# Group norm moments aggregated chunk by chunk, mean squares on ScalarE, sum completed in TensorE's average

## What is computed

```python
diff = a1 - lam * a2
out = einsum(diff, v)                      # B, H, T, 64
mean = mean(out, axis=(1, 3)); var = var(out, axis=(1, 3))   # per sequence and head
out = (out - mean) * rsqrt(var + EPS) * gn_w + gn_b
out = out.reshape(B, T, 1024) * (1 - LAMBDA_INIT) @ Wo
x = layernorm(x + out); ...                # then the experts
```

## Time and profile before

| | |
|---|---|
| median of 3 runs | 2042.45 us |
| the runs | 2035.61 to 2043.52 us |
| the profiled execution's own time | 2053.17 us |
| its span in the trace | 2051.3 us |
| mean granted TensorE clock | 0.925 |
| batches 1 to 7 in the attention stage | about 160 us each |

### The profile page before, as it was taken

How to read it: one execution, slowest core, us unless ns; L and a number is a source line. 1 busy time by engine, 2 the same in 40 slices (tenths; PEclk the granted TensorE clock), 3 DMA queues, 4 the chain that set the end, 5 groups by cost and what they waited for, 6 DMA issues and landing times. The chain is left out here.

```text
span 2051.3 us, 36805 instructions
## 1 busy us (share of the span) xinstructions
PE 1706.9 (83%) x9698; PEld 1270.7 (62%) x9699; DVE 1389.8 (68%) x3225; ACT 1166.7 (57%) x3378; POOL 585.5 (29%) x480
## 2 busy tenths in 40 slices
PE   4578899899889889889889889783999999999600
PEld 3355666666656656656665666442999999999600
DVE  2589888888888988888888898734333333333385
ACT  2478788688777877777877877822222222222133
POOL 2232232432331331242242242011633342100173
PEclk8799999999999999999999999975999999999855
DMA  7975574574474474575466565113543344433285
GB/s 253 294 210 141 137 194 121 161 213 114 143 209 134 143 216 125 137 215 153 136 206 165 145 189 150 54 69 140 165 125 118 92 133 151 128 102 93 78 270 194
DMA packets 142469, 318.74 MB, mean 155 GB/s; under 512 B 16720, under 2 KB 19408, under 8 KB 140272
## 3 DMA queue, kind: packets, MB, share of 16 engines
q1 hardware_dynamic: 112272, 238.98, 41.6%
q0 software_dynamic: 15072, 50.74, 7.4%
q10 hardware_dynamic: 14976, 27.27, 3.5%
HBM read 215.21 MB, written 109.05 MB: 158 GB/s over the span
## 5 line engine op out<-in xcount | busy, mean ns | idle before, releaser
L806 ACT ACTIVATE expd<-S,neg_max 128x128 f32<-128x128 f32 (+3 forms) x1024 | 531.5, 536 | 161.2 <-DVE neg_max L961 159.0
L961 DVE TENSOR_REDUCE neg_max<-S 128x2 f32<-128x768 f32 (+3 forms) x384 | 399.9, 1041 | 164.9 <-PE S L650 155.9
L992 DVE SCALAR_TENSOR_TENSOR mixed<-expd,rho 128x384 f32<-128x384 f32 (+3 forms) x512 | 335.4, 675 | 0.0
L646 PE MATMUL S<-kT,qT 128*128 128x256 f32 (+2 forms) x1024 | 278.5, 374 | 20.7 <-ACT expd L806 11.2
L818 ACT ACTIVATE probsT<-PTp 128x512 f32<-128x512 f32 (+2 forms) x384 | 205.2, 534 | 114.7 <-PE PTp L661 112.8
L661 PE MATMUL PTp<-ident,mixed 128*128 128x128 f32 x1280 | 215.8, 284 | 53.5 <-DVE mixed L992 49.0
L1372 ACT ACTIVATE xT_hi<-xTp 128x512 fp32r<-128x512 f32 x72 | 43.1, 599 | 358.0 <-DVE yo L1553 352.4
L646 PEld LDWEIGHTS S<-kT,qT 128*128 128x128 f32 x1024 | 163.8, 194 | 123.2 <-issue 83.1
L700 PE MATMUL tail<-wo,ctxT 128*128 128x512 f32 x480 | 225.6, 594 | 0.5
L538 POOL TENSOR_TENSOR swapped<-swapped,rope_t 128x512 f32<-128x512 f32 x80 | 104.1, 1301 | 420.7 <-DVE swapped L954 420.7
L806 ACT ACTIVATION_READ_ACCUMULATOR expd<-S,neg_max 128x1 f32 x1024 | 217.2, 212 | 0.0
(11 more groups left out here) (224 smaller groups left out, 3675.1 us busy)
## 6 DMA issues: line engine op xcount, KB each, us to landing
qT<-parts_rows SPq DMA_DIRECT2D x256, 256.0 KB, 4.3
parts_rows<-parts SPq DMA_DIRECT2D x160, 256.0 KB, 2.3
wqk<-wqk_split SPq DMA_DIRECT2D x75, 512.0 KB, 6.1
xin<-expert_in_rows SPq DMA_DIRECT2D x72, 256.0 KB, 3.0
expert_out_rows<-yo ACTq DMA_DIRECT2D x72, 256.0 KB, 3.2
kT<-parts_rows SPq DMA_DIRECT2D x64, 256.0 KB, 4.5
x<-in_x SPq DMA_DIRECT2D x8, 1024.0 KB, 7.2
x_rows<-x SPq DMA_DIRECT2D x8, 1024.0 KB, 7.3
```

The source lines that it names most:

```text
L646: nc.tensor.matmul(S[s % 2][:, k * slot:k * slot + w], qT[kv % 2][:, 2 * h + c, i * P:(i + 1) * P], kT[kv][:, c, 0:w], start=(k % per_bank ...
L806: ex = nc.scalar.activation(expd[s % 3][:, k * slot:k * slot + w], S[s % 2][:, k * slot:k * slot + w], ACT.Exp, bias=neg_max[s % 3][:, k:k ...
L961: nc.vector.tensor_reduce(neg_max[s % 3][:, 0:k], v, AX, ALU.max, negate=True).then_inc(max_ready, 1)
L992: ins = nc.vector.scalar_tensor_tensor(out=mixed[sl % 3][:, a * 256:a * 256 + w], in0=e2, scalar=rr[:, i, h:h + 1], in1=e1, op0=ALU.mult, ...
```

## The change

VectorE aggregates each chunk one step after its statistics (new `chunk_moments`, at steps 25, 38, 42, 42, 44, 44, and 7 and 8 of the next batch), with a wait on the count of statistics so far; at step 8 it stands ahead of the rotation. The copy, the square and the sum on VectorE are gone, and `st2` with them. ScalarE squares the eight means at step 8 behind its exponentials (`sq`), and TensorE averages twice into the same 16 columns of PSUM: `st` (means and variances), then `sq` added onto the columns of the variances. `mean of (var + mean^2)` is what was averaged before.

```diff
@@ tensor, tail_task
                 if kind == "gn":
-                    pe.wait_ge(st_ready, b + 1)
+                    pe.wait_ge(sq_ready, b + 1)
                     tail_bank_free(pe, b, ending[0], *task)
-                    nc.tensor.matmul(tail[:, 0:2 * FC], avg[:], st2[:].rearrange("p c s -> p (c s)"),
-                                     start=True, stop=True).then_inc(tail_full, 1)
+                    both = tail[:, 0:2 * FC]
+                    nc.tensor.matmul(both, avg[:], st[:].rearrange("p c s -> p (c s)"), start=True, stop=False)
+                    nc.tensor.matmul(both.rearrange("p (c s) -> p c s", s=2)[:, :, 1], avg[:], sq[:],
+                                     start=False, stop=True).then_inc(tail_full, 1)
@@ scalar
+                if kind == "gsq":
+                    act.wait_ge(st_ready, b + 1)
+                    nc.scalar.activation(sq[:], st[:, :, 0], ACT.Square).then_inc(sq_ready, 1)
+                    return
...
-            mine = {10: [("gn", 0)], DONE + 1: [("ln", 0)], DONE + 11: [("wt", 0)]}
+            mine = {8: [("gsq", 0)], 10: [("gn", 0)], DONE + 1: [("ln", 0)], DONE + 11: [("wt", 0)]}
@@ vector
+            CHUNK_ORDER = sorted(range(FC), key=lambda c: (CHUNK_STEPS[c], c))
+
+            def chunk_moments(b, c):
+
+                n = CHUNK_ORDER.index(c)
+                dve.wait_ge(bn_step, FC * b + n + 1)
+                apart(dve)
+                ins = nc.vector.bn_aggr(st[:, c, :], bn[:, c, :])
+                if n == FC - 1:
+                    ins.then_inc(st_ready, 1)
...
-                if what == "gstats":
-                    dve.wait_ge(bn_step, FC * (b + 1))
-                    apart(dve)
-                    for c in range(FC):
-                        ins = nc.vector.bn_aggr(st[:, c, :], bn[:, c, :])
-                    link(b, ins)
-
-                    nc.vector.tensor_copy(st2[:, :, 0], st[:, :, 0])
-                    link(b, nc.vector.tensor_tensor(st2[:, :, 1], st[:, :, 0], st[:, :, 0], ALU.mult))
-                    nc.vector.tensor_tensor(st2[:, :, 1], st2[:, :, 1], st[:, :, 1], ALU.add).then_inc(st_ready, 1)
...
@@ vector, body, between the ratio and the rotation of a step
+                    for c in CHUNK_ORDER:
+                        if CHUNK_STEPS[c] + 1 == s:
+                            chunk_moments(b, c)
+                        elif CHUNK_STEPS[c] + 1 == s + UB and not first:
+                            chunk_moments(b - 1, c)
@@ vector, end
+                for c in CHUNK_ORDER:
+                    if CHUNK_STEPS[c] + 1 >= UB:
+                        chunk_moments(b - 1, c)
```

More of the change, by code:

```diff
@@ L218, in attention_block @@
         st = sb("st", [P, FC, 2])
-        st2 = sb("st2", [P, FC, 2])
+        sq = sb("sq", [P, FC])
         gst = sb("gst", [P, FC, 2])
@@ L297, in attention_block @@
         st_ready = sem("st_ready")
+        sq_ready = sem("sq_ready")
         bn_step = sem("bn_step")
@@ L1007, in chunk_stats @@
                 nc.vector.bn_stats(out=bn[:, c, :], in_=ctxT[par][:, c, :]).then_inc(bn_step, 1)
+            CHUNK_ORDER = sorted(range(FC), key=lambda c: (CHUNK_STEPS[c], c))
[6 more added lines that the diff above has]
+                    ins.then_inc(st_ready, 1)
             links = [0]
-            LINKS = 19
+            LINKS = 17
             def link(b, ins):
@@ L1021, in tail_work @@
                 tail = tail_bank((SOURCE[what], j), ending[0]) if what in SOURCE else None
-                if what == "gstats":
-                    dve.wait_ge(bn_step, FC * (b + 1))
-                    apart(dve)
-                    for c in range(FC):
-                        ins = nc.vector.bn_aggr(st[:, c, :], bn[:, c, :])
-                    link(b, ins)
-                    nc.vector.tensor_copy(st2[:, :, 0], st[:, :, 0])
-                    link(b, nc.vector.tensor_tensor(st2[:, :, 1], st[:, :, 0], st[:, :, 0], ALU.mult))
-                    nc.vector.tensor_tensor(st2[:, :, 1], st2[:, :, 1], st[:, :, 1], ALU.add).then_inc(st_ready, 1)
-                elif what == "gvar":
+                if what == "gvar":
                     dve.wait_ge(tail_full, tail_count(b, "gn", 0))
@@ L1104, in tail_work @@
                     nc.vector.tensor_tensor(wts[:, here, 1], ed[:], wts[:, here, 0], ALU.mult)
-            mine = {8: [("gstats", 0)], 10: [("gvar", 0)], 11: [("gaffine", 0)], DONE + 2: [("ln", 0)],
+            mine = {10: [("gvar", 0)], 11: [("gaffine", 0)], DONE + 2: [("ln", 0)],
                     DONE + 10: [("route", 0)], DONE + 11: [("picks", 0)], DONE + 12: [("slots", 0)], DONE + 13: [("places", 0)]}
```

## The result

| | before | changed |
|---|---|---|
| median of 5 runs | 2039.87 us | 2017.06 us |
| the runs | 2035.61 to 2043.52 | 2015.63 to 2024.58 |
| ratio, 95% interval | | 0.9898 (0.9873 to 0.9922) |
| span of the profiled execution | 2051.3 us | 2019.3 us |
| mean granted TensorE clock | 0.925 | 0.937 |

The 5 runs of the kernel before include the 3 shown above. The change makes the kernel 1.0% faster, 22.8 us by the medians; the forecast was 2029, the range began at 2017. Beside other kernels on another chip the changed kernel ran once more, 2031.84 against 2051.04 us, ratio 0.9918 (0.9893 to 0.9942). Both intervals hold a gain of 16 to 22 us.

What follows compares the result with a forecast made beforehand. TensorE, 83% busy, was taken as the bound, waiting 27.9 us in all for the statistics sum. 18.9 - 4.5 - 1.5 + 0.3 = 13.2 us: 2053.2 becomes 2040.0 profiled, 2042.45 becomes 2029; range 2017 to 2039.

Steps and rivals of the forecast that it cites:

- What bounds, and the step removed: TensorE waits 3.46 us for VectorE's group norm at step 8, held by GpSimd; removing it starts the scaled context 2.6 us sooner.
- VectorE, ScalarE, TensorE at steps 8 and 9: Scaled context at about 566.0; square 0.25 us, ScalarE idle 1.5; both averages hide before the projection at about 566.2.
- that rival: ScalarE's square at step 8 needs another activation table, two loads of 1.28 us; gain 4.8 us, time 2038, chance 0.02.
- The collision: Step 9's mix or ratio collides with GpSimd's second operation; step 10's maxima start at about 569.3, gaining 2.7 us, not 3.8.
- Steps 8 to 13: These steps of a batch take 17.1 us in place of 19.8; 2.7 us in seven batches, 18.9.
- TensorE's next gap: Idleness before the scores of step 13, waiting for ScalarE's exponentials of step 11, grows from 0.34 to about 1.3 us.
- I assume it in three batches of four: Half clock at step 13, 1.39 us a batch, in 5.25 batches in place of two; 4.5 us given back.
- Moved aggregates: 48 aggregates standing alone at steps 25, 38, 42 and 44 cost between nothing and 8.6 us; 1.5 us taken.
- more than five batches of it: Sign of being wrong: half-clock stretches in more than five batches at steps where batch 3 had none.
- Last tail: The last wait of 3.8 us shortens little, as no GpSimd operation holds VectorE there; 0.3 us gained.
- the first rival, the clock that stays up: No half clock at step 13, and batches 4 and 7 gain 1.39 us too; gain 20.5 us, time 2022, chance 0.14.
- the chances: Five sixths of the forecast's spread lies beyond 10 us: faster 0.66, within 0.5% 0.27, slower 0.07; forecast itself 0.60.

Runs made afterwards that it cites:

- order experiment: Kernel before with its whole statistics task (eight aggregates, copy, square, sum) moved ahead of the rotation of step 8; ratio 0.9962, 2042 against 2049 us.
- aggregates left at step 8: Kernel before with square on ScalarE and sum in TensorE's average, all eight aggregates still at step 8 behind the rotation; ratio 0.9886.
- aggregates spread: The change with aggregates one step behind their chunk, but copy, square and sum left on VectorE and a single average; ratio 0.9939.
- fourfold experiment: The change with every chunk's aggregate taken four times instead of once; steps 8 to 13 took 17.23 us, attention stage ended at 1325.1 us.
- late ratio: The change with the ratio of step 9 put behind the row maxima of step 10; ratio 0.9888.
- late ratio and early parts together: The change with step 9's ratio behind step 10's maxima and step 5's rotation split one step after it instead of two; 2028.16 us, ratio 0.9900.
- early parts: The change with the high and low parts of step 5's rotation split one step after it instead of two; ratio 0.9919.

## Why the prediction came out as it did

**What bounds, and the step removed: right.** The wait fell from 3.46 to 0.25 us, and that the small instructions were held and not long is shown by the order experiment alone (0.17 us each). The copy, held for 0.82 us, has one SBUF input; the rule quoted in the prediction is on two, and covers the sum alone.

**VectorE, ScalarE, TensorE at steps 8 and 9: right, nearly to the tenth.** Scaled context 3.3 us after the maxima of step 8 (561.61 - 558.32), forecast 566.0 - 562.72 = 3.3. The square took 0.20 us, in the bounds of 0.20 and 0.30, and the idleness behind it 1.67, forecast 1.5. The two averages took 0.58 us and hid in front of the shuffle's end. No table load came with the square, so that rival falls; a switch of tables, where there is one, took 1.29 us from the load's start to the square root's (568.04 to 569.33), not the 2.7 us that the prediction names beside it.

**The collision: right.** Maxima of step 10 started 6.49 us after those of step 8 (564.81 - 558.32), forecast 6.6. The Trainium skill's rule ("SBUF — State Buffer", Who interferes with whom), that the later of the two waits for the whole of the other, agrees with these rows: ratio 1.24 us and GpSimd's operation 1.71 us behind a mix that came first, mix 1.18 where GpSimd came first (aggregates left at step 8). Where the two start within 0.02 us of each other the rows do not tell which came first: in batch 1 the mix has the earlier start by 0.01 us and was held, 1.69 us.

**Steps 8 to 13: 17.1 forecast, 17.03 measured.** The place of TensorE's next gap was wrong. I put 1.3 us before the scores of step 13, behind ScalarE. In five of seven batches it was 1.6 to 1.9 us before the scores of step 12, behind the transfer of the turned queries, which I had not looked at: in the kernel before, waits for it were rare. It did no harm because both bounds end within tenths of each other.

**What failed: "I assume it in three batches of four".** The term was half clock after step 13, 4.5 us given back. It came in none of seven batches; in the repeated run one batch had a stretch at step 12, which cost 0.4 us; and the two stretches that the kernel before had are gone: steps 13 to 16 take 9.8 us throughout (10.0 in batch 7), 2.7 us less in sum than before. The term was +2.7 and not -4.5. Batch 4's gap of 1.34 us was too little to argue from: in the change gaps of 1.6 to 1.9 us were followed by full clock, and batch 2 had 1.30 us at the very place of the prediction, before the scores of step 13, and kept its clock. Over all twelve executions twelve batches had a gap of 1.30 to 1.35 us there, and in five of them, two of these in the kernel before, the clock fell. What else decides it is not settled. It does happen: in the eleven executions of kernels other than the one before, 6 of 77 batches took 10.9 to 11.3 us there, two of them with aggregates spread.

**Moved aggregates: 1.5 us taken, about 0.1 us per batch by the fourfold experiment.** Between change and kernel before, steps 24 to 47 take no more in batches 2 to 6; in sum over seven batches they take 1.0 us more, from the 1.6 us of half clock at step 39 of batch 1. The prediction had no term for such a stretch; it named more than five batches of it as a sign of being wrong, and there was one. **Last tail: right.** From the scaled context to the copy of the averages it took 3.62 in place of 3.91 us, 0.3.

**The sum.** Steps 8 to 13 in seven batches 18.5 (18.9 forecast), steps 13 to 16 2.7 (-4.5), steps 24 to 47 -1.0 (-1.5, for the aggregates), and 1.3 in all other steps, 1.2 of it in batch 0, which differed by as much either way among the other executions: with rounding 21.4, by which the last row maxima start sooner. The tail's 0.3 come behind them. This is the first rival, the clock that stays up (20.5 us, 2022), to which I gave 0.14; the forecast's 13.2 us were 9.6 short of the 22.8 measured by the medians. The range held the measured median by 0.06 us, 2017.06 against 2017, which is luck: the first runs alone lie from 2015.63 to 2024.58. One step in the chances was off as well: of a gain of 13.2 us, 6 either side, about three quarters lie beyond 10 us if it is spread evenly, not five sixths.

## What to carry to other kernels

Every very small VectorE instruction here that took about a microsecond, a sum, a ratio, a copy, was waiting for GpSimd. So look at GpSimd's timeline beside such a row, and before moving work to another engine try to put it ahead of whatever starts GpSimd. Ask of every gain which wait will end last in its place, the transfers included: here two bounds lay together, so that each removal alone was worth 0.15 us or nothing and both were worth 1.0 us per batch. Forecast from stretches that repeat in every batch, and price a clock stretch that came in two of seven as just that.

## What was unexpected

- The combine stage of one kernel took 104.7 and 116.5 us in two executions, at 243 and 219 GB/s. A single profile of this kernel can be 12 us off for that alone; the cause is open.
- Half clock behind the average, after a gap of 1.5 us, cost at most 0.3 us per batch and not 1, because ScalarE's chain and the transfer end later than TensorE either way.
- Two operations tie within 0.03 us at the mix of step 9, and either engine may win: with late ratio the step from 9 to 10 took 1.7 us in four batches and 2.8 in three.
- Two averages into one PSUM tile, the second onto every other column, took 0.24 and 0.34 us from start to start, the second until the projection, which also waits for the shuffle's end. Their rows last 0.39 and 0.37 us, so no penalty for the stride can be seen at eight columns.
- The clock fell at step 39 in batches where the kernel before held it, at 1.6 us each, in every other kernel; with late ratio and early parts together it did so in three of six. The cause is open.
